# Two-layer decoder on one core: the norm between stages made batch by batch inside the attention in front of it

## The reference, cut to what matters

```python
x = x + L0_attn(layernorm(x))                     # 16 heads, causal
x = x + L0_xattn(layernorm(x), ctx)               # 16 heads, 375 context rows
x = x + L0_ffn(layernorm(x))                      # rmsnorm, group attention, rmsnorm, 32 routed experts
x = x + L1_attn(layernorm(x))                     # 32 heads, rotary, learned bias, sink
x = x + L1_xattn(layernorm(x), ctx)               # rmsnorm of it first; gated output
x = x + L1_ffn(layernorm(x))                      # 2048 hidden, as 8 "experts" of 256

def _layernorm(x, axis=-1, eps=1e-05):
    m = jnp.mean(x, axis=axis, keepdims=True)
    v = jnp.var(x, axis=axis, keepdims=True)
    return (x - m) / jnp.sqrt(v + eps)
def rmsnorm(x, w, eps=EPS):
    var = jnp.mean(x * x, axis=-1, keepdims=True)
    return x * jax.lax.rsqrt(var + eps) * w
```

## Time and profile before

| | us |
|---|---|
| three runs | 2422.39, 2433.91, 2434.66 |
| their median | 2433.91 |
| the profiled execution | 2430.01 |
| its span in the trace | 2428.2 |
| PE busy | 2208.1 (91%) |
| DVE busy | 1312.2 (54%) |
| ACT busy | 925.1 (38%) |
| POOL busy | 984.8 (41%) |

### The profile page before, as it was taken

One profiled execution on the slowest core, in us unless ns is written; L12 is line 12 of the kernel. 1 busy time (PEld: TensorE's weight loads), 2 busy tenths in 40 slices (PEclk: granted clock), 3 DMA queues, 4 the chain that ended last, 5 costly groups with the idle time before them and its releaser, 6 DMA issues. The chain is left out here.

```text
span 2428.2 us, 41046 instructions
## 1 busy us (share of the span) xinstructions
PE 2208.1 (91%) x15152; PEld 1588.1 (65%) x15152; DVE 1312.2 (54%) x2358; ACT 925.1 (38%) x1630; POOL 984.8 (41%) x787
## 2 busy tenths in 40 slices
PE   7889999697999999889999998697879999979997
PEld 6658777476888887643333333286657777759997
DVE  4554666557777777553333332686762666643333
ACT  1332222244445444236666665114533332322221
POOL 2333554356655564315666665253433110012220
PEclk9989999799999999989999999899999999979999
DMA  3002010121111110376666879620021000011110
GB/s 124 24 26 84 27 40 1 66 74 57 61 45 65 53 57 9 118 266 158 141 147 140 241 197 279 158 81 25 2 83 43 26 14 27 1 52 53 52 52 31
DMA packets 56909, 194.38 MB, mean 80 GB/s; under 512 B 8260, under 2 KB 8516, under 8 KB 49860
## 3 DMA queue, kind: packets, MB, share of 16 engines
q1 hardware_dynamic: 36660, 147.44, 17.9%
q0 software_dynamic: 17280, 38.94, 8.2%
q10 hardware_dynamic: 2784, 5.51, 0.8%
HBM read 158.70 MB, written 33.16 MB: 79 GB/s over the span
## 5 line engine op out<-in xcount | busy, mean ns | idle before, releaser
L2100 PE MATMUL bank<-m_ring,m_bT 128*64 x576 | 266.6, 606 | 3.5 <-DMA m_ring<-in_m_w 3.4
L2102 PE MATMUL bank<-m_upper,m_bT 128*64 128x512 f32 x576 | 266.6, 607 | 0.0
L2018 DVE SCALAR_TENSOR_TENSOR m_prod<-bank,m_slot_rows,m_silu 64x256 f32<-64x256 f32 x144 | 69.6, 483 | 274.0 <-ACT m_silu L1765 271.4
L2100 PEld LDWEIGHTS bank<-m_ring,m_bT 128*64 128x64 f32 x576 | 73.9, 138 | 142.4 <-issue 142.4
L1736 POOL DMA_INDIRECT m_sum<-m_yb,m_idx x72 | 102.8, 1428 | 143.0 <-DVE m_yb L2029 110.1
L1820 ACT ACTIVATE m_upper<-m_ring 128x1024 f32 x144 | 143.4, 1046 | 2.5 <-issue 2.4
L856 ACT ACTIVATE y_att_p_rows<-bank,y_att_n_top 112x375 f32<-112x375 f32 x128 | 71.6, 572 | 190.1 <-DVE y_att_n_top L898 190.1
L2129 PE MATMUL bank<-m_ring,m_aT 128*64 x288 | 135.4, 592 | 0.7 <-DVE m_aT L2035 0.7
L2131 PE MATMUL bank<-m_upper,m_aT 128*64 128x512 f32 x288 | 135.4, 593 | 0.0
L225 PE MATMUL bank<-f_hT_hi,f_w_hi 128*128 128x448 f32 x288 | 111.3, 387 | 10.9 <-DVE f_q L1391 3.1
L853 ACT ACTIVATE x_att_pT<-x_att_s_clip 125x336 f32<-125x336 f32 x128 | 55.3, 485 | 159.8 <-DVE x_att_s_clip L892 159.8
(11 more groups left out here) (498 smaller groups left out, 6197.4 us busy)
## 6 DMA issues: line engine op xcount, KB each, us to landing
m_ring<-in_m_w SPq DMA_DIRECT2D x32, 1536.0 KB, 7.9
f_raw<-in_f_wq SPq DMA_DIRECT2D x64, 256.0 KB, 2.6
z_raw<-in_z_w SPq DMA_DIRECT2D x7, 1536.0 KB, 6.3
f_att_wo_raw<-in_f_wo SPq DMA_DIRECT2D x16, 512.0 KB, 3.7
m_sum<-m_slot_rows SPq DMA_DIRECT2D x4, 2048.0 KB, 18.3
x_c_raw<-in_ctxT SPq DMA_DIRECT2D x8, 752.0 KB, 4.7
y_c_raw<-in_ctxT SPq DMA_DIRECT2D x8, 752.0 KB, 4.3
a_raw<-in_a_wqk SPq DMA_DIRECT2D x8, 256.0 KB, 4.1
```

The lines of the kernel that those rows point to most:

```text
L2100: pe.matmul(ps_gu[u % 2][0:HP, :], bT[:, n % 2, k, 0:HP], ring[:, bass.ds(slot + at, D)], start=(k == 0), stop=(k == KC - 1))
L2102: o = pe.matmul(ps_gu[u % 2][HP:P, :], bT[:, n % 2, k, HP:P], upper[:, n % 2, at:at + D], start=(k == 0), stop=(k == KC - 1))
```

## The change

Four norms (x, f, y, z) are given to the attention in front of them as `following` and are made there for batches 0 to 6 (`ready = B - 1`). The norms of a and b have no attention directly in front and keep their old form. In detail:

- `row_stats` and `moments` follow each batch's addition: `bn_stats`, `bn_aggr` and the variance of that batch alone on DVE.
- `roots` on POOL: one `pow` of one column a batch; for "ln_rms" five operations of one column.
- `rows` on DVE: `h`, and `y` for "ln_rms". In `self_attention` batch b - 1 is taken at the end of batch b, before `add(b)`; in `cross_attention` batch b - 2 is taken in the middle of batch b (x: before `finish(b - 1)`; y: before `add(b - 1)`), and batch 6 at the end, before `rows_of(7)`.
- In the next block PE turns batches 0 to 6 at once (28 transposes), makes the first product, and only then turns batch 7. DVE makes the moments of batch 7, the low parts of batches 0 to 3 with the low parts of the first weights in between (no longer POOL), those of 4 to 6, the rows of batch 7 and its low part.
- For a and b `front` is 4: PE turns batches 0 to 3, makes the first product, then turns batches 4 to 7.
- The first weights of x, y and z are loaded during the attention in front (`load_ahead`), those of f as before.
- In `experts` the first product waits for two of the three weight pieces.
- The rows (`norm_rows`), `x_raw`, `y_raw`, `z_raw` and `y_gate` get fixed places in SBUF, and `f_x2` lives from the start.

```diff
+    def moments(self, dve, b):
+        dve.wait_ge(self.stats_done, b + 1)
+        dve.bn_aggr(self.mv[:, b, :], self.g.stats[:, b, :]).then_inc(self.aggr_done, 1)
+        dve.wait_ge(self.aggr_done, b + 1)
+        dve.tensor_scalar(self.var[:, b:b + 1], self.mv[:, b, 1:2], 1e-5, None, ALU.add).then_inc(self.var_done, 1)
+
+    def roots(self, pool, b):
...
+        pool.wait_ge(self.var_done, b + 1)
+        pool.tensor_tensor(rstd, self.var[:, one], power, ALU.pow).then_inc(self.rstd_done, 1)
+        if self.kind == "ln_rms":
...
+    def rows(self, dve, b):
+        dve.wait_ge(self.rstd_done, b + 1)
+        dve.tensor_scalar(self.h[:, b, :], self.src[:, b, :], self.mv[:, b, 0:1], self.rstd[:, b:b + 1],
+                          ALU.subtract, ALU.mult).then_inc(self.h_done, 1)
+        if self.kind == "ln_rms":
+            dve.wait_ge(self.rrms_done, b + 1)
+            dve.wait_ge(self.h_done, b + 1)
+            dve.scalar_tensor_tensor(self.y[:, b, :], self.h[:, b, :], self.rrms[:, b:b + 1], self.w,
+                                     ALU.mult, ALU.mult).then_inc(self.y_done, 1)
...
     def vector(self, dve):
+        if self.ready:
+            for b in range(self.ready, B):
+                self.moments(dve, b)
+            pieces = len(self.early.raws)
+            for b in range(HB):
+                self.low(dve, b)
+                if b < pieces:
+                    self.early.split_one_low(dve, b, self.early_hi, self.early_lo)
+            for b in range(HB, self.ready):
+                self.low(dve, b)
+            for b in range(self.ready, B):
+                self.rows(dve, b)
+                self.low(dve, b)
+            return
...
     def scalar(self, act):
+        if self.arrived:
+            pieces = len(self.early.raws)
+            act.wait_ge(self.arrived, 16 * pieces)
+            for b in range(B):
+                if b < pieces:
+                    act.activation(self.early.his[b], self.early.raws[b], ACT.Copy).then_inc(self.early_hi, 1)
+                transposed_high(b)
+            return
...
-            norm.tensor(pe)
+            norm.transposes(pe, 0, norm.front)
             for t in range(NH):
                 pe.wait_ge(norm.lo_done, HB * (t + 1))
                 for u in range(2):
                     pe.wait_ge(norm.early_lo, u + 1)
                     unit(0, u, t)
+                    if t == 0 and u == 0:
+                        norm.transposes(pe, norm.front, B)
...
             for n in range(N):
+                if n >= SG + 2 and (n - 2) % SG == 0:
+                    following.roots(pool, (n - 2) // SG - 1)
...
                 if ends:
+                    if b:
+                        following.rows(dve, b - 1)
                     add(b)
                     row_stats(b)
...
                 for j in range(4, 8):
                     clip_scores(b, j)
+                if b >= 2:
+                    following.rows(dve, b - 2)
                 if b:
                     finish(b - 1)
...
                 turned(b, 4)
                 turned(b, 5)
+                if b >= 2:
+                    following.rows(dve, b - 2)
                 if b:
                     add(b - 1)
                     finish(b - 1)
...
             heads_out(B - 1)
+            following.rows(dve, B - 2)
             rows_of(B - 1)
...
                 if first:
-                    pe.wait_ge(norm.early_lo, NP_)
+                    pe.wait_ge(norm.early_lo, 2)
                     pe.wait_ge(norm.lo_done, HB)
                 pe.wait_ge(lo_done, NP_ * (e + 1))
                 gate_up(e, slot, 0)
+                if first:
+                    norm.transposes(pe, norm.front, B)
+                    pe.wait_ge(norm.early_lo, NP_)
```

More of the change, by code:

```diff
@@ L123, with __init__ @@
 class Norm:
-    def __init__(self, ctx, nc, g, name, src, kind, eps2=0.0, w=None, keep=None, early=None, ahead=(), first=None):
-        def sb(n, shape):
-            return ctx.enter_context(nc.sbuf_tensor(f"{name}_{n}", shape, F32))
-        sem = ctx.enter_context(semaphores(nc, name))
-        self.g, self.src, self.kind, self.eps2, self.w, self.early, self.ahead, self.first = (
-            g, src, kind, eps2, w, early, ahead, first)
-        self.h = keep if keep is not None else sb("h", [S, B, D])
-        self.y = self.h if kind == "ln" else sb("y", [S, B, D])
-        self.mv, self.var, self.rstd, self.ssq, self.ms, self.rrms = (
-            sb(n, s) for n, s in (("mv", [S, B, 2]), ("var", [S, B]), ("rstd", [S, B]), ("ssq", [S, B]), ("ms", [S, B]),
-                                  ("rrms", [S, B])))
+    def __init__(self, nc, g, name, src, kind, eps2=0.0, w=None, keep=None, rows=None, ready=0, loads=(),
+                 arrived=None):
+        self.loads, self.arrived = loads, arrived
+        self.stack = ExitStack()
+        sem = self.stack.enter_context(semaphores(nc, name))
+        self.g, self.src, self.kind, self.eps2, self.w, self.ready = g, src, kind, eps2, w, ready
+        self.front = ready or HB
+        self.y = rows
+        self.h = keep if kind == "ln_rms" else rows
+        self.mv, self.var, self.rstd, self.ssq, self.ms, self.rrms = g.norm
+        self.ahead, self.first = (), None
         (self.stats_done, self.aggr_done, self.var_done, self.rstd_done, self.h_done, self.ssq_done, self.ms_done,
@@ L209, in scalar, with transposes @@
             transposed_high(b)
-    def tensor(self, pe):
+    def transposes(self, pe, at, to):
         g, ready = self.g, self.h_done if self.kind == "ln" else self.y_done
-        if self.first:
+        if self.first and at == 0:
             pe.wait_ge(self.first.consts_in, 16)
-        for b in range(B):
+        for b in range(at, to):
             pe.wait_ge(ready, b + 1)
@@ L558, in _ @@
                     pool.tensor_tensor(x[:, n, :], x[:, n, :], wo_bias, ALU.add).then_inc(bo_done, 1)
+            for b in range((N - 3) // SG, B - 1):
+                following.roots(pool, b)
         @block.scalar
@@ L636, in row_stats @@
                 dve.wait_ge(add_done, b + 1)
-                dve.bn_stats(g.stats[:, b, :], x[:, b, :])
+                following.row_stats(dve, b)
+                if b < following.ready:
+                    following.moments(dve, b)
             if bias_in:
@@ L2590, in program @@
                 weights = weight_pair(w, "a")
-                norm = Norm(w, nc, g, "a_norm", x, "ln", first=first, early=first_pair(a["a_wqk"], weights),
-                            ahead=small_loads)
+                norm = Norm(nc, g, "a_norm", x, "ln", rows=norm_rows).begin(w, first_pair(a["a_wqk"], weights), small_loads, first)
                 project(nc, g, norm, "a_proj", a["a_wqk"], 2 * KC, qk, weights, bias=pvec[:, 0:8],
@@ L2595, in program @@
             causal = g.const("causal")[0:S].unsqueeze(1).broadcast_to([S, 4, S])
+            x_raw = nc.alloc_sbuf_tensor_at("x_raw", [P, 2, KC * P], F32, offset=ROWS_AT - PAIR)
+            x_norm = Norm(nc, g, "x_norm", x, "ln", rows=norm_rows, ready=B - 1, arrived=x_raw_in,
+                          loads=[(x_raw[:, u, :], a["x_wq"][u]) for u in range(2)])
             self_attention(nc, g, "a_att", x, qk[:, 0:KC], qk[:, KC:2 * KC], v, 16, 32 ** -0.5, lambda sg, j: causal,
-                           a["a_wo"], a["spread4"], wo_bias=g.row("a_bo")[0:S])
+                           a["a_wo"], a["spread4"], wo_bias=g.row("a_bo")[0:S], following=x_norm)
         with ExitStack() as st:
@@ L2657, in mask_to_bias @@
                     dve.tensor_scalar(y_bias[:, :], y_mask_row[:, :], 1.0, -NEG, ALU.subtract, ALU.mult)
[L2659 removed]
+                h = w.enter_context(nc.sbuf_tensor("b_norm_h", [S, B, D], F32))
+                norm = Norm(nc, g, "b_norm", x, "ln", rows=h).begin(
+                    w, first_pair(a["b_wqk"], weights),
                           ahead=[(bias[:, :, :], a["b_bias"], b_bias_in),
```

178 lines of the change are left out of this document (107 added, 71 removed).

## The result

The change made the kernel **slower by 0.28%**: the median of 20 runs is 2433.7 us against 2426.6 for the kernel before, ratio 1.0028 with a 95% interval of 1.0017 to 1.0039. Timed once more as an experiment, the changed kernel stood at 1.0041 (1.0026 to 1.0057). The sign is settled, and it is the other one. One of the five executions of the experiment `e7_together` took 3292.2 us at a granted clock of 0.63 and is left out of its figures.

A forecast was written before the change was run, and what follows sets the result against it. PE, busy 91% of the span, was taken as the bound. Starts gain 24.7, less 6.4 (a, b), 5.6 and 2.9 (second and first cross attention): 9.8 off 2430.0 gives 2420.2 us; own range 2414 to 2427, over the cases 2408 to 2434.

The forecast's parts named there:

- Starts of x, f, y, z: From first norm operation to first product in four stages: gains of 2.9, 6.6, 8.3 and 6.9, together 24.7 us.
- First cross attention: Added DVE work makes the copy for PE 0.2 us late in six batches, last batch pays 1.7: loss 2.9, range 0 to 11.
- h, y and the moments: First cross attention: these DVE operations push the copy `keys_values(b + 1, 2)` back by 1.7 us.
- the last batch: First cross attention's end: no projection to hide behind, so the whole 1.7 us is paid.
- Second cross attention: No slack before `turned(b, 6)`: 0.87 us for batches 2 to 7, 0.40 for batch 1; loss 5.6, floor 0.
- a and b: Stage starts: 16 transposes behind the first product cost 1.6 us each, low clock 1.6 each; loss 6.4, at least 3.2.
- f and z: Starts of f and z: the range allowed 3 us either way for the clock at a, b, f, z.
- rival B: First products run at the low clock in x and y too: 2 x 1.6 us more, 2423.4; chance 0.08.
- Rival A: PE makes up its small cross-attention waits and the clock stays up at a, b, f, z: 2410; chance 0.2.
- Rival C: POOL's chain of small operations delays the second self attention, 17 us: 2437; chance 0.1.
- Rival D: A forgotten wait keeps PE's 28 transposes behind DVE: 2430 or more; chance 0.05.
- The sum itself: Start of x: first product at 5.0 instead of 8.5, transposes on PE's path 0.4 to 0.5: gain 2.9 us.

The follow-up runs named there:

- e7_together: All repairs together (rows moved in both cross attentions, a and b's transposes ahead, PE filled, z's clearing moved) against the kernel before: 2395.8 us, 0.9855.
- second profiles: Controls: the changed kernel and the kernel before, each profiled again unedited; y's first product to z's 0 took 353.5 us after, 341.5 before.
- The experiment: Changed kernel with rows, addition and moments moved in the second cross attention, against the kernel before: 2424.8 us, 0.9983.

## Why the prediction was wrong

- **Starts of x, f, y, z: right.** Forecast 27.8 us off the four distances, measured 29.5. The sum that the change could win was read rightly.
- **First cross attention: wrong, and it alone turned the sign.** The step that failed is "h, y and the moments: 1.3 + 0.4 = 1.7 us in front of `keys_values(b + 1, 2)`". The term that was mis-sized is the row, 0.69 where it measured 1.71, and the stretch of x's update behind it, 0.89, had no term at all. I took 0.69 from an addition with only one of its inputs in SBUF, and did not ask what POOL, busy 115 of 253 us in this very stage, reads at that moment. The shift was 3.58 us, so PE waited 1.96 us instead of 0.2. The second half of the miss is that I priced the wait as a wait; behind three of five the clock fell as well. 19.8 us in place of 3.4. For the last batch I had written that the whole shift is paid, and it was: 3.3 us, of a shift of 3.58 and not of 1.7. The range I had given for this term, 0 to 11, came from the queue alone.
- **Second cross attention: mechanism right.** The shift in front of `turned(b, 6)` is 0.87 us, as forecast: from the output row's start to `turned` 3.64 instead of 2.77 us. The stretch grew by 8.5 us in place of 6.5 with the batch-7 transposes counted; against the second profiles 12.0, part of it clock. The experiment shows that the place costs, not the work.
- **a and b:** transposes behind the product, 16 in 1.5 us, and a low clock at both first products, as forecast. At b the reason was partly another one: the clock did not fall while PE stood, it had not yet risen when the 16 transposes ended, and in three of the experiments (x's rows earlier, x's update first, z's clearing) it had, and b's product began at full clock. The loss in b is 4.6 and 5.4 for 3.2; in a it does not show in the sum, because the attention's last output rows ran at full clock (3.69 us) where they had 6.70 at the low one before: luck, and the second profiles give +0.8.
- **f and z:** low clock there, as forecast; at z for 16 passes, about 6 us of which less than 3 are lost, against 8 passes before. x's first product fell to the low clock too, 0.7 us after it started, and y's kept it, as in most runs. That is half of rival B, but the clock fell behind PE's standing and not because only transposes had run.
- **Rival A** fell: PE did not catch up in the cross attentions. **Rival C** fell: POOL's small operations took 0.55, 0.19, 0.19, 0.22 and 0.57 us. **Rival D**: the change did what it says. The case that came true, a stretched operation in front of PE's next copy, was in none of them. The sum itself is off by 0.1 at x, where 8.5 - 5.0 - 0.5 is 3.0; nothing hangs on it.

## What to carry to other kernels

Price an inserted operation by its neighbours on the other engines as well as by its shape: here a VectorE operation with two inputs in SBUF took about twice its time beside GpSimd's additions, so put such a one where its engine waits anyway. Where PE has no slack, a late copy costs the wait, and when the clock falls behind it nearly as much again (here 2.2 and 1.5 us a batch); an idle place a few operations earlier in the same queue turned a loss of 20 us into none. Where PE must stand for two microseconds, filling work whose result nobody reads kept its clock, for a few microseconds in all.

## What the runs showed of the hardware

- A 112x512 `scalar_tensor_tensor` with two SBUF inputs: 0.75 us alone, 1.42 to 1.71 beside POOL's 448-column additions, 0.75 beside POOL's memsets. POOL's second addition went from 1.14 to 1.48 beside the stretched update.
- Waits of PE of 1.8 to 2.0 us were followed by some 3 us at 0.50 in 13 of 24 cases (the ten for kT in the two profiles of the change, six ahead of x's first product, eight ahead of y's), with nothing in the program telling which; five waits of 0.8 us were followed by none.
- With 14 to 22 transposes in gaps of 2 to 3 us the granted clock was 1.00 in the first product behind them, at x, f, b, y and z. At b and z it rose from 0.50 to 1.00 while PE ran nothing but transposes.
